# Three of four parts of G and of Bf as split products, the first in plain fp32, with the remainders on GpSimd

## The reference

```
w_eff = dequant(quant_to_8_levels(W + 0.5*B@A, per 128-block scale)) + 0.5*B@A
x = x + attn(x @ w_eff.T, Wqkv, bqkv, Wo, bo)            # one head, d = 128
h = x @ A_e.T                                            # 8 experts, rank 16
gates = softmax(top2(x @ Wr.T + 5 * onehot(language)))
c = x @ W.T + 2 * sum_e gates_e * (h_e @ B_e.T)
x = x + c @ (scale * (q - zero_point)).T + bias
```

## Time and profile before

| | us |
|---|---|
| runs | 110.79, 111.05, 112.26 |
| median | 111.05 |
| the profiled execution | 112.07 |
| its span, first to last instruction | 110.3 |
| PE busy in the span | 104.8 (95%) |
| DVE, ACT, POOL busy | 71.6, 52.7, 11.6 |

### The profile page before, as it was taken

The page is one execution under the profiler, slowest core; times in us unless marked ns, Lnnn a source line. Parts: engine busy times, 40 slices in busy tenths (PEclk is TensorE's granted clock), DMA queues, the critical chain, the costliest instruction groups (busy, mean ns, idle before and its releaser), DMA issues.

```text
span 110.3 us, 1419 instructions
## 1 busy us (share of the span) xinstructions
PE 104.8 (95%) x500; PEld 83.4 (76%) x500; DVE 71.6 (65%) x168; ACT 52.7 (48%) x96; POOL 11.6 (10%) x26
## 2 busy tenths in 40 slices
PE   4979999999999999999999999999999999999980
PEld 4957944445966888999988888788989888888850
DVE  0099999999999999970899714202864911491441
ACT  4339899999996850181702226734108224002000
POOL 4000000000000000019500008700000400000000
PEclk9996799999999999999999999999999999999999
DMA  2999999930000000000000000000000370000072
GB/s 56 226 346 326 408 396 416 404 103 3 0 0 0 0 0 0 0 3 6 0 0 0 0 0 0 0 0 0 6 0 0 116 265 0 6 3 0 0 285 95
DMA packets 4391, 9.57 MB, mean 87 GB/s; under 512 B 736, under 2 KB 992, under 8 KB 4384
## 3 DMA queue, kind: packets, MB, share of 16 engines
q1 hardware_dynamic: 4384, 9.48, 24.2%
HBM read 7.38 MB, written 2.10 MB: 86 GB/s over the span
## 4 chain that ended last, share of the span: by engine, by line
PE 88%; DMA 4%; DVE 3%; ACT 2%; DVEq 1%; issue 0%
PE psum L824 19%; PE psum L826 19%; PE psum L825 18%; PE psum L857 13%; PE psum L845 8%; DMA lora<-in_lora 4%; PE psum L879 3%; PE psum L971 2%; PE psum L950 2%; PE psum L965 2%; ACT moe L444 1%; DVE xT_lo L554 1%; PE psum L957 1%; PE psum L873 1%; PE psum L978 1%; DVE neg_max L734 1%
## 5 line engine op out<-in xcount | busy, mean ns | idle before, releaser
L857 PE MATMUL psum<-q_i,moe 128*128 128x512 f32 x32 | 14.2, 597 | 0.0
L621 DVE COPY_PREDICATED cond_work<-cond_work,levels 128x1024 f32<-128x1024 int32 x10 | 13.5, 1355 | 0.1
L824 PE MATMUL psum<-G_hi,xT_hi 128*128 128x512 f32 x32 | 12.8, 399 | 0.0
L826 PE MATMUL psum<-G_hi,xT_lo 128*128 128x512 f32 x32 | 12.5, 391 | 0.0
L825 PE MATMUL psum<-G_lo,xT_hi 128*128 128x512 f32 x32 | 12.5, 390 | 0.0
L349 ACT ACTIVATE cond_work<-cond_n,cut_bias 128x1024 f32<-128x1024 f32 x10 | 11.4, 1147 | 0.7 <-DVE cond_n L658 0.6
L857 PEld LDWEIGHTS psum<-q_i,moe 128*128 128x128 f32 x32 | 5.8, 190 | 6.5 <-issue 6.5
L845 PEld LDWEIGHTS psum<-hlT,xT 128*128 128x128 f32 x64 | 9.1, 215 | 1.0 <-issue 0.9
L503 POOL TENSOR_TENSOR xT_lo<-xT,xT_hi 128x1024 fp32r<-128x1024 f32 x2 | 4.7, 2392 | 47.4 <-ACT xT_hi L319 47.4
L824 PE MATMUL psum<-xT_hi,split_b_hi 128*128 128x512 f32 x24 | 9.6, 401 | 0.0
L845 PE MATMUL psum<-hlT,xT 128*128 128x136 f32 x64 | 9.6, 307 | 0.0
(11 more groups left out here) (151 smaller groups left out, 216.5 us busy)
## 6 DMA issues: line engine op xcount, KB each, us to landing
out<-cond_work SPq DMA_DIRECT2D x7, 256.0 KB, 2.1
cond_n<-in_cond_w SPq DMA_DIRECT2D x2, 512.0 KB, 6.3
xT<-in_x_t SPq DMA_DIRECT2D x2, 512.0 KB, 7.4
q_i<-in_q_t SPq DMA_DIRECT2D x4, 256.0 KB, 7.0
moe<-in_moe_w SPq DMA_DIRECT2D x4, 256.0 KB, 7.2
xT<-in_x_t SPq DMA_DIRECT2D x1, 1024.0 KB, 12.3
wqkv_n<-in_wqkv SPq DMA_DIRECT2D x1, 768.0 KB, 10.2
hlT<-in_hl_t SPq DMA_DIRECT2D x1, 272.0 KB, 5.6
```

The lines of the kernel that those rows point to most:

```text
L621: dve.copy_predicated(half(level, h), beyond[n % len(beyond)].bitcast(I32), levels[:, j + 1:j + 2].to_broadcast([P, 2 * C])).then_inc(pick ...
L824: pe.matmul(out_ap, l_hi, r_hi, start=first, stop=False)
L826: return pe.matmul(out_ap, l_lo, r_hi, start=False, stop=last)
L857: pe.matmul(psum[i][:, :], moe[:, o, s], w_ffn[:, o, :], start=(o == 0), stop=False)
```

## The change

Parts 1, 2 and 3 of G and of Bf become split products; part 0 of each stays plain fp32. Their hi halves are made on ACT (`moe_hi`, `w_hi`), w_ffn's remainder on DVE (`w_lo`), W's and B's remainders on POOL. Around it much is moved:

- On POOL, each behind a wait on the count of picks done: the normalisation of the second half, its start level, and the remainders of x, Wo and Wqkv, which DVE or ACT made before.
- The picks read their level from PSUM bank 7, where a second copy of the levels is written. Bf goes to bank 4, and y_x(1) is taken before y_x(0).
- The LoRA input comes in two loads, one issued by ACT. The warm-up has 26 transposes. The LoRA product runs its four hi*hi matmuls first, and DVE makes the LoRA remainders after the cuts, no longer before them.

```diff
-    WARM_UP = 20
+    WARM_UP = 26
...
+            act.dma_start(lora[0:RANK, 1, :], lora_in[0:RANK, 1, :]).then_inc(loaded["lora_a"], 16)
+            for n, name in enumerate(("lora_b", "lora_a")):
+                act.wait_ge(loaded[name], 16)
                 rounded(lora_hi[:, n, :], lora[0:RANK, n, :], lora_hi_ready)
...
+            def moe_hi(o):
+                act.wait_ge(loaded[f"moe{o}"], 16)
+                rounded(split_a_hi[:, o, :], moe[:, o, :], moe_hi_ready)
+            def w_hi(o):
+                act.wait_ge(w_ready, o + 1)
+                rounded(split_b_hi[:, o, :], w_ffn[:, o, :], w_hi_ready)
...
-            def normalise(h):
-                act.wait_ge(wd_ready, h + 1)
-                for g in range(h * GROUPS // 2, (h + 1) * GROUPS // 2):
...
             beyond_cut(0, 0)
             beyond_cut(1, 0)
+            hl_raw(0, 4)
+            moe_hi(1)
+            w_hi(1)
             beyond_cut(2, 0)
-            hl_raw(0, 4)
             beyond_cut(3, 0)
+            moe_hi(2)
+            beyond_cut(4, 0)
+            w_hi(2)
+            moe_hi(3)
+            beyond_cut(5, 0)
+            w_hi(3)
+            beyond_cut(6, 0)
             x_hi(0)
-            beyond_cut(4, 0)
-            set_level(1)
-            beyond_cut(5, 0)
-            beyond_cut(6, 0)
-            normalise(1)
-            beyond_cut(0, 1)
...
+            pool.wait_ge(picked, 1)
+            moe_rest(1)
+            pool.wait_ge(wd_ready, 2)
+            pool.wait_ge(inv_scale_ready, 1)
+            pool.wait_ge(picked, 2)
+            pool.tensor_tensor(blocks(1), blocks(1), inv_scale[:, GROUPS // 2:GROUPS].unsqueeze(2).to_broadcast(
+                [P, GROUPS // 2, P]), ALU.mult).then_inc(norm_late_ready, 1)
+            pool.wait_ge(picked, 4)
+            moe_rest(2)
+            pool.wait_ge(picked, 5)
+            moe_rest(3)
+            pool.wait_ge(picked, 6)
+            pool.tensor_copy(half(level, 1), levels[:, 0:1].to_broadcast([P, 2 * C])).then_inc(level_late_set, 1)
+            pool.wait_ge(expb_hi_ready, 1)
+            pool.wait_ge(w_eff_ready, 2)
+            rest(expb_lo[:, 1:CT, :], expb[:, 1:CT, :], expb_hi[:, 1:CT, :], expb_lo_ready)
+            pool.wait_ge(woT_hi_ready, 1)
+            rest(woT_lo, woT[:, :, :], woT_hi, woT_lo_ready)
+            x_lo(0)
+            wqkv_rest(0)
...
+            pool.wait_ge(picked, CUTS + 5)
+            x_lo(1)
             x_lo(2)
             x_lo(3)
...
+            def w_lo(o):
+                dve.wait_ge(w_hi_ready, o)
+                dve.tensor_tensor(split_b_lo[:, o, :], w_ffn[:, o, :], split_b_hi[:, o, :], ALU.subtract)\
+                   .then_inc(w_lo_ready, 1)
...
                 dve.copy_predicated(half(level, h), beyond[n % len(beyond)].bitcast(I32),
-                                    levels[:, j + 1:j + 2].to_broadcast([P, 2 * C])).then_inc(picked, 1)
+                                    psum[EARLY][:, j + 1:j + 2].to_broadcast([P, 2 * C])).then_inc(picked, 1)
...
             def G_product(o):
-                pe.wait_ge(w_ready, o + 1)
-                pe.wait_ge(loaded[f"moe{o}"], 16)
+                if o == 0:
+                    pe.wait_ge(w_ready, 1)
+                    pe.wait_ge(loaded["moe0"], 16)
+                else:
+                    pe.wait_ge(w_lo_ready, o)
+                    pe.wait_ge(moe_lo_ready, o)
...
-                    pe.matmul(psum[i][:, :], moe[:, o, s], w_ffn[:, o, :], start=(o == 0), stop=False)
+                    if o == 0:
+                        pe.matmul(psum[i][:, :], moe[:, o, s], w_ffn[:, o, :], start=True, stop=False)
+                    else:
+                        three(psum[i][:, :], split_a_hi[:, o, s], split_a_lo[:, o, s],
+                              split_b_hi[:, o, :], split_b_lo[:, o, :], False, False)
...
-            for o in range(CT):
-                mm = pe.matmul(psum[7][:, :], expb[:, o, :], w_ffn[:, o, :], start=(o == 0), stop=(o == CT - 1))
+            pe.wait_ge(hl_raw_ready, 1)
+            pe.matmul(psum[4][:, :], expb[:, 0, :], w_ffn[:, 0, :], start=True, stop=False)
+            pe.wait_ge(expb_lo_ready, 1)
+            for o in range(1, CT):
+                mm = three(psum[4][:, :], expb_hi[:, o, :], expb_lo[:, o, :], split_b_hi[:, o, :],
+                           split_b_lo[:, o, :], False, o == CT - 1)
```

More of the change, by code:

```diff
@@ L310, in half, with blocks @@
             return ap[:, 2 * h:2 * h + 2, :].rearrange("p t n -> p (t n)")
+        def blocks(h):
+            return cond_n[:, 2 * h:2 * h + 2, :].rearrange("p t (g n) -> p (t g) n", n=P)
         def nth(j, h):
@@ L400, in _ @@
             w_eff_hi(1)
-            beyond_cut(2, 1)
             hl_raw(1, 5)
-            wqkv_round(0)
-            wqkv_round(1)
+            wqkv_round(3)
+            beyond_cut(3, 1)
             x_hi(1)
+            act.wait_ge(Bf_done, 1)
+            act.activation(Bf_hi[:, :], psum[4][:, :], ACT.Copy, scale=EXPERT_SCALE).then_inc(Bf_hi_ready, 1)
             act.wait_ge(woHL_done, 1)
@@ L549, in alone, with lora_rest @@
                 dve.wait_ge(dve_step, mark(ins))
-            for n in range(2):
+            def lora_rest(n):
                 dve.wait_ge(lora_hi_ready, n + 1)
@@ L609, in w_delta @@
                 dve.tensor_tensor(cond_n[:, t, :], cond_n[:, t, :], delta[:, t, :], ALU.add).then_inc(wd_ready, 1)
-            def blocks(h):
-                return cond_n[:, 2 * h:2 * h + 2, :].rearrange("p t (g n) -> p (t g) n", n=P)
             def pick(j, h):
@@ L664, in _ @@
             pick(1, 0)
+            w_delta(1)
             pick(2, 0)
+            w_lo(1)
             w_full(2)
             pick(3, 0)
-            w_delta(1)
+            w_full(3)
             pick(4, 0)
-            w_full(3)
+            w_lo(2)
             pick(5, 0)
+            w_lo(3)
             pick(6, 0)
@@ L674, in _ @@
             w_eff(1)
-            x_lo(0)
             pick(0, 1)
-            woT_rest()
+            pick(1, 1)
             for i in range(CT):
                 G_rest(i)
-            pick(1, 1)
             w_eff_lo(0)
@@ L830, in _ @@
             for _ in range(WARM_UP):
-                pe.transpose(psum[7][:, 0:P], ident[:, :], ident[:, :])
+                pe.transpose(psum[6][:, 0:P], ident[:, :], ident[:, :])
+            pe.wait_ge(lora_hi_ready, 2)
+            for o in range(CT):
+                s = slice(o * P, (o + 1) * P)
+                pe.matmul(psum[o][:, :], lora_hi[:, 0, s], lora_hi[:, 1, :], start=True, stop=False)
             pe.wait_ge(lora_lo_ready, 2)
@@ L836, in _ @@
                 s = slice(o * P, (o + 1) * P)
-                three(psum[o][:, :], lora_hi[:, 0, s], lora_lo[:, 0, s], lora_hi[:, 1, :], lora_lo[:, 1, :], True, True)\
-                    .then_inc(delta_done, 1)
+                pe.matmul(psum[o][:, :], lora_lo[:, 0, s], lora_hi[:, 1, :], start=False, stop=False)
+                pe.matmul(psum[o][:, :], lora_hi[:, 0, s], lora_lo[:, 1, :], start=False, stop=True)\
+                  .then_inc(delta_done, 1)
             def x_hl(part, bank, batches=None, base=0):
@@ L916, in _ @@
                     pe.wait_ge(xT_lo_ready, 1)
-                y_x(0, range(c, c + 1))
-            pe.wait_ge(hl_raw_ready, 2)
-            y_x(1)
+                    pe.wait_ge(hl_raw_ready, 2)
+                y_x(1, range(c, c + 1))
+            pe.wait_ge(Bf_lo_ready, 1)
+            y_x(0)
             pe.wait_ge(woHL_ready, 1)
@@ L928, in _ @@
             M_product(3)
[L929 removed]
+            pe.wait_ge(picked, HALVES * CUTS)
             y_x(3)
```

108 lines of the change are left out of this document (57 added, 51 removed).

## The result

The changed kernel takes **115.73 us** (median; 115.62 to 115.95), the kernel before on the same chip 111.66 (110.79 to 113.87): ratio 1.039, 95% interval 1.030 to 1.049. The ratio leaves out one slow execution of the kernel before (113.87), without which its median is 111.05. The profiled execution took 115.95 us; its span is 113.8, so 2.15 us lie outside the span, where it was 1.8 before.

The account below looks back on a forecast made before the run. PE bounds the kernel, with DVE full beside it. G's end moves +3.45 us (30.9 against 27.45), Bf gives back 0.5: +2.95 on the profiled 112.07 makes 115.0 us, range 113.2 to 117.0.

Parts of the forecast that it names:

- PE's saving: In G twelve products go from 0.86 to 0.70 us, saving 1.9; in Bf three, saving 0.5; together 2.4 if operands are there.
- DVE reaches w_lo(1) at 18.9: On DVE, picks, dequantisations and the second half's weight sum come first, so it reaches w_lo(1) only at 18.9 us.
- The normalisation, 17.8 to 20.2: On POOL, the second half's normalisation starts once the weight sum has ended and takes 2.39 us.
- w_lo(1) blocked, done at 20.9: On DVE, w_lo(1) cannot overlap POOL's normalisation, waits until 20.2 us, then takes 0.69.
- The rival without blocking: w_lo(1) runs beside the normalisation, so parts 1 and 2 of G start 1.3 us earlier: 113.7 us; chance 12%.
- PE idle for 4.1 us from 16.75: In G, PE ends part 0 at 16.75 us or earlier and waits for w_lo(1) until 20.9.
- Part 1 in 2.8 us, then 1.2 of wait: In G, part 1 runs at 0.23 per matmul to 23.7 us; PE then idles 1.2 until w_lo(2) ends at 24.9.
- the first rival: Half clock after PE's wait: part 1 of G at 1.2 GHz, 1.6 us more, 116.6 us; chance 25%.
- Nothing waits behind G, the block is moved: Behind G, the remainders of Bf, Wo, x and w_eff come in time, so the attention moves as a block.
- Quick picks: DVE's picks take half their time, bringing G's end 2.5 us earlier: 112.5 us, no change; chance 8%.
- PE never waits: w_lo(1) is ready by 16.75 us, so PE gets the full 2.4 us saving: 109.7 us; chance 5%.
- The basis: The forecast adds to the profiled execution's 112.07 us, not subtracting the 1.0 above the median 111.05; otherwise the answer is 114.0.

Follow-up runs that it names:

- experiment 2: The changed kernel with POOL's normalisation of the second half held back until w_lo(1) is done: 115.28 us, ratio 1.039 to the kernel before.
- experiment 6: The changed kernel, all three parts split, with only the order on DVE, ACT and GpSimd edited, each w_lo earlier: 113.32 us, ratio 1.024 to the kernel before.
- experiment 9: The kernel of experiment 6 with x's second remainder, Bf's remainder and the bias instructions reordered: 111.86 us, ratio 1.006 to the kernel before.
- experiment 5: The changed kernel with only parts 2 and 3 of G and Bf split, and DVE, ACT and GpSimd work reordered: 110.35 us, ratio 0.997 to the kernel before.
- experiment 3: The changed kernel with 36 unused transposes on PE between parts 0 and 1 of G: 114.75 us, ratio 1.035 to the kernel before.
- experiment 7: The kernel before with one edit, 26 warm-up transposes for 20: 111.58 us, ratio 1.006; its profiled execution, at full clock throughout, took 110.79.
- experiment 4: The changed kernel with G and Bf all plain fp32, without the copies and subtractions only splitting needs, other moves kept: 112.49 us, ratio 1.014 to the kernel before.
- experiment 1: The changed kernel with w_lo(1) moved directly behind the second pick on DVE: 116.52 us, ratio 1.048 to the kernel before.
- experiment 8: The changed kernel with the picks reading their level from SBUF again, not PSUM: 123.3 us, ratio 1.114 to the kernel before.

## Why the prediction was right, step by step

The forecast of 115.0 was 0.95 us under the profiled execution (115.95) and 0.7 under the median. The mechanism, PE waiting for w_lo(1), is shown by experiments 2, 6 and 9, which each take away a part of it. That the number came so close is in part luck, as the part on part 1 below says.

- **PE's saving**, 12 x 0.16 and 3 x 0.16: right. The split products take 0.23 at full clock; experiment 5 ended G 1.1 us earlier with eight of them, and Bf gave 0.5 back.
- **First pick at 13.6**: 13.43. **DVE reaches w_lo(1) at 18.9**: 18.66.
- **The normalisation, 17.8 to 20.2**: 17.65 to 19.55. The term is mis-sized: I took 2.39 from the row of a plain subtraction, and with a broadcast factor it took 1.90.
- **w_lo(1) blocked, done at 20.9**: blocked, done at 20.09; freed, it takes 0.67 (experiment 2). The rival without blocking would have seen the 1.43 as 0.69.
- **PE idle for 4.1 us from 16.75**: 4.26 from 15.9. Both ends were 0.8 earlier: the early slow stretch was gone, as the bound had it, and gave nothing but an earlier arrival at the wait.
- **Part 1 in 2.8 us, then 1.2 of wait**: this is the step that failed. Part 1 took 5.5 us at 1.2 GHz, to 25.64, and no wait followed. By my sum part 2 would have begun 24.9, and it began 0.7 later. That is the first rival (116.6), whose mechanism came true. Its price was 1.6; the row gives 2.7 - 1.2 = 1.5 on G's end, and experiment 3, which takes the half clock away, 1.0. The 0.8 by which w_lo(1) came earlier than forecast took back half of the 1.5, so that the time fell between the forecast and the rival. That the forecast missed by no more than 0.95 is luck to this extent: two errors of opposite sign. I gave the rival 25% although the row that spoke for it was in the table; 4 us of idle should have made it the likeliest.
- **Nothing waits behind G, the block is moved**: right here, since G was late. It is not so when G is in time (experiment 6: 1.6 us of waits).
- **Quick picks** and **PE never waits**: picks took 1.32 to 1.39, PE waited. Both fell.
- **The basis.** I added 2.95 to 112.07, the profiled execution of before, and did not take off the 1.0 between it and the median. That was right. That execution had a slow stretch that most do not have, but the stretch lies ahead of G: from G's end on it takes 84.6 us, the undisturbed one of experiment 7 84.7. The forecast is G's end at 30.9, and it is the same 115.0 from either: +2.95 on the disturbed execution, +4.2 on the undisturbed one. Profiled against profiled, the loss on the undisturbed one was 115.95 - 110.79 = 5.2. The missing 0.95 are 0.7 in G (31.63 for 30.9) and 0.2 behind it. For that 0.2 I had nothing in the sum, and no term for the time outside the span, which grew by 0.35. Measured by the medians the loss is 4.1 to 4.9.

What stays open: which parts of the 1.6 us of experiment 4 are order, the start of G, the longer warm-up and the time outside the span; why most executions with the longer warm-up alone are slower; and why some executions of the kernel before have the early slow stretch.

## What to carry to other kernels

A cheaper product pays only if its operands are ready when the engine comes: add up the queue of the engine that makes them, up to each instruction, before counting the saving, and leave the first parts plain so that they cover the rest. When one wait is removed, ask where the next one stands; here the second remainder, then the remainders of x and Bf each took over. A loss is quoted against an execution without disturbances: the same forecast time is +2.95 against one with an early stretch at half clock and +4.2 against one without. A wait in the row costs more than its idle time, so compare the same instruction in both traces. Where a change is many moves, run each alone: here the longer warm-up gained nothing and may have cost 0.7.

## What the runs showed of the hardware

- **DVE and GpSimd on SBUF.** A subtraction with two SBUF inputs beside a GpSimd operation: 1.43 us for 0.69. A dequantisation with one SBUF tensor, int32, and factors from SBUF: 1.10, 1.19 and 1.53 for 0.54 (experiments 1, 4 and 8), so it is held up too. A pick with one input in PSUM: 1.29 to 1.40 in every trace, GpSimd busy or not. A pick with both in SBUF: 1.34 to 1.41, but GpSimd stops, 5.61 for 1.3 to 1.6; or, where GpSimd was first, 3.05 (experiment 8).
- **PE's clock.** Waits of 3.5, 3.9 and 4.3 us in G each came with a stretch at 1.2 GHz, some 6.8 us long in the profiled executions (in the change 18.9 to 25.7, so it began 3 us into the wait). It is not the same in every execution: two of the change's four have a mean granted clock of 0.970, two of 0.982, and the latter are 0.2 us faster. Waits of 0.35 to 1.2 us in G came with none. But in the profiled execution of before a stretch of 3.4 us (9.1 to 12.5) followed a wait of only 0.7. 36 transposes in the wait of 4.3 kept the clock at 2.4 GHz (experiment 3). The Trainium skill (TensorE: Matmul & The Clock Gate, Part 4: PE-mode transpose) says that the full clock doesn't engage for transposes, which do not count as busy in the same way; experiment 3 speaks against that for these fp32 ones.
- **GpSimd.** Two-input operation on 1024 fp32 columns: 2.4 us plain, 1.90 with a broadcast second input; a copy of 1024 columns 1.04 in experiments 4, 5, 6 and 9, and 1.41 in the change.
